# Router logits from four column tiles of TensorE, with the router's weights stationary and one turn of the result

## The reference, cut to what matters

```python
h = _layernorm(x) * (1 + ca) + sa
x = x + ga * mamba(h)                      # a scan over 2048 steps for 512 x 16 states
h = _layernorm(x) * (1 + cb) + sb
s_raw_MN = h @ Wg_DN                       # router logits, 8 a token: what the change touches
routed = softmax(s_raw_MN[:, :7]); shared = softmax(s_raw_MN[:, 7:])
mask = one_hot(top_k(routed, 1)); sel = routed * mask
gates = concatenate([sel / sum(sel), shared / sum(shared)])
y = sum over n of gates[:, n] * ((silu(h @ W1_n[:, H:]) * (h @ W1_n[:, :H])) @ W2_n)
x = x + gb * y
```

## Time and profile before

| what | value |
|---|---|
| time, median of 3 | 2514.27 us |
| the profiled execution's own time | 2508.63 us |
| its span, first to last instruction | 2506.6 us |
| mean granted TensorE clock | 0.904 |
| VectorE busy | 1929.8 us (77%) |
| GpSimd busy | 1955.7 us (78%) |
| TensorE busy | 2176.9 us (87%) |
| ScalarE busy | 1360.7 us (54%) |
| one chunk, mean of 14 | 117.0 us |

### The profile page before, as it was taken

The page is one execution under the profiler, slowest core; times in us unless marked ns, Lnnn a source line. Parts: engine busy times, 40 slices in busy tenths (PEclk is TensorE's granted clock), DMA queues, the critical chain, the costliest instruction groups (busy, mean ns, idle before and its releaser), DMA issues. The chain is left out here.

```text
span 2506.6 us, 31126 instructions
## 1 busy us (share of the span) xinstructions
PE 2176.9 (87%) x7664; PEld 1058.5 (42%) x7665; DVE 1929.8 (77%) x2060; ACT 1360.7 (54%) x2440; POOL 1955.7 (78%) x840
## 2 busy tenths in 40 slices
PE   8769898988989898999898898989857649999997
PEld 3214343443434343434343443434323335566654
DVE  2799999999999999989999999999897162222222
ACT  3666666667575766666666667576644232222221
POOL 1999889898989898988989898989897014555553
PEclk9868989898989898988989898989878869999999
DMA  5443242424232333424242424232321062222221
GB/s 154 135 110 94 76 103 67 101 68 113 81 92 74 96 82 87 116 79 105 68 103 69 101 68 111 81 94 77 89 68 42 24 208 76 85 84 83 87 85 45
DMA packets 149401, 224.39 MB, mean 90 GB/s; under 512 B 48227, under 2 KB 85617, under 8 KB 145138
## 3 DMA queue, kind: packets, MB, share of 16 engines
q1 hardware_dynamic: 135858, 182.44, 28.0%
q0 software_dynamic: 13376, 40.12, 5.2%
HBM read 99.48 MB, written 31.47 MB: 52 GB/s over the span
## 5 line engine op out<-in xcount | busy, mean ns | idle before, releaser
L1023 POOL TENSOR_TENSOR hs<-hs,c_rep 128x2048 f32<-128x2048 f32 x256 | 1154.5, 4528 | 37.3 <-ACT state L767 37.2
L863 DVE TENSOR_TENSOR_SCAN hs<-dA,state,hs 128x512 f32<-128x512 f32 x768 | 931.1, 1264 | 21.0 <-ACT dA L747 16.7
L747 ACT ACTIVATE dA<-d_rep,a 128x512 f32<-128x512 f32 x1024 | 690.0, 686 | 427.7 <-DVE hs L863 423.2
L1016 POOL TENSOR_TENSOR hs<-u_rep,b_rep 128x2048 f32<-128x2048 f32 x96 | 435.5, 4536 | 88.9 <-PE bank L517 88.9
L850 DVE TENSOR_TENSOR hs<-u_ps,b_rep 128x2048 f32<-128x2048 f32 x160 | 360.9, 2272 | 8.0 <-issue 4.8
L488 PE MATMUL bank<-n,w1s 128*128 128x512 f32 x512 | 268.4, 661 | 68.0 <-DVE delta L831 39.2
L863 DVE TENSOR_TENSOR_SCAN hs<-dA,hs 128x512 f32<-128x512 f32 x256 | 294.0, 1202 | 19.7 <-ACT dA L747 18.6
L517 PE MATMUL bank<-hs,spread 128*32 128x512 f32 x2048 | 280.3, 696 | 32.1 <-POOL hs L1023 28.0
L1408 DVE TENSOR_TENSOR hid<-z,sg 128x512 f32<-128x512 f32 x70 | 48.4, 692 | 298.1 <-ACT sg L1386 298.1
L1326 PE MATMUL z<-w1r,hT 128*128 x560 | 260.5, 608 | 3.4 <-issue 2.4
L446 PE MATMUL bank<-xin,w_in 128*128 128x512 f32 x512 | 245.1, 619 | 9.2 <-ACT xin L600 9.2
(11 more groups left out here) (173 smaller groups left out, 2531.9 us busy)
## 6 DMA issues: line engine op xcount, KB each, us to landing
d_rep<-delta SPq DMA_DIRECT2D x1024, 64.0 KB, 2.0
u_rep<-us SPq DMA_DIRECT2D x384, 64.0 KB, 2.0
b_rep<-bc_rows SPq DMA_DIRECT2D x64, 256.0 KB, 4.7
c_rep<-bc_rows SPq DMA_DIRECT2D x64, 256.0 KB, 7.8
xres<-in_x SPq DMA_DIRECT2D x16, 512.0 KB, 3.6
token_rows<-xpad SPq DMA_DIRECT2D x32, 256.0 KB, 2.3
token_rows<-xres SPq DMA_DIRECT2D x16, 512.0 KB, 3.0
xin<-in_x SPq DMA_DIRECT2D x15, 512.0 KB, 9.5
```

The costliest lines, as they stand in the source:

```text
L747: nc.scalar.activation(dA[:, u % ABANK, :], d_rep[:, q, :], ACT.Exp, scale=t["a"][:, u:u + 1]).then_inc(da_ready, 1)
L863: nc.vector.tensor_tensor_scan(hs[:, s % RING, g, :], dA[:, u % ABANK, :], hs[:, s % RING, g, :], state[:, u:u + 1] if m else 0.0, ALU.mul ...
L1016: nc.gpsimd.tensor_tensor(hs[:, s % RING], u_rep[:, i % UBUF, :].unsqueeze(1).to_broadcast([P, NG, T]), b_rep[:, par, :].rearrange("p (g t ...
L1023: nc.gpsimd.tensor_tensor(hs[:, s % RING, :, :], hs[:, s % RING, :, :], c_rep[:, par, :].rearrange("p (g t) -> p g t", g=NG), ALU.mult).th ...
```

## The change

- `GL` now holds the router's 8 columns stationary and lets 128 tokens of `h2T` move. Tile tt of the tokens goes to column tile tt of the array (32 columns, of which 8 are used), and its logits come out on partitions 32 tt to 32 tt + 7, one partition for each expert, one column for each token. It is 8 matmuls as before, ordered with the feature halves outside. The bank's other partitions hold what was in them.
- ScalarE copies all 128 partitions x 128 columns of this to `lgT`, the first 128 columns of `hid`'s part 1.
- `GT` is a new TensorE group: one transpose of `lgT` gives tokens on partitions. It stands between `B` 0 and `B` 1 in the plan.
- ScalarE copies from it the 4 x 8 columns of `lg`, at `evict[10][3]` ahead of `B` 1, where `logits_kept` is signalled now; the copy at the old place, `evict[10][0]`, signals `lgT_ready`.
- `GT` reads through ScalarE, so the list of such groups has 29 members, and every one after `GT` gets the other of the two banks.

```diff
+        lgT = hid[:, 1, 0:P]
+        lgT_made, lgT_ready = sem("lgT_made"), sem("lgT_ready")
         plan:
-            9: [(('GL', 0), -1), (('RB', 1), -1), (('SUM', 1), 0), (('B', 0), -1), (('B', 1), -1), (('B', 2), -1), (('DB', 0), 1), (('B', 3), -1), (('DT', 2), 1)],
+            9: [(('GL', 0), -1), (('RB', 1), -1), (('SUM', 1), 0), (('B', 0), -1), (('GT', 0), -1), (('B', 1), -1), (('B', 2), -1), (('DB', 0), 1), (('B', 3), -1), (('DT', 2), 1)],
         evict:
-            10: [[(('GL', 0), -1), (('L0', 0), 1), (('RB', 1), -1)], [], [(('B', 0), -1)], [(('B', 1), -1)]],
+            10: [[(('GL', 0), -1), (('L0', 0), 1), (('RB', 1), -1)], [], [(('B', 0), -1)], [(('GT', 0), -1), (('B', 1), -1)]],
-        ACT_READS = ("T", "XS", "CV", "RS", "XP", "DT", "T2", "RB", "GL", "B")
+        ACT_READS = ("T", "XS", "CV", "RS", "XP", "DT", "T2", "RB", "GL", "GT", "B")
         made: "GL": logits_made -> "GL": lgT_made, "GT": logits_made
         kept: "GL": logits_kept -> "GL": lgT_ready, "GT": logits_kept
         TensorE:
                 elif kind == "GL":
                     pe.wait_ge(h2T_ready, KD * f + KD)
-                    for tt in range(TT):
-                        for k in range(KD):
-                            last = nc.tensor.matmul(ps_[:, tt * NEXP:(tt + 1) * NEXP], h2T[:, k, tt * P:(tt + 1) * P], t["wg"][:, k, :],
-                                                    start=(k == 0), stop=(k == KD - 1))
+                    for k in range(KD):
+                        for tt in range(TT):
+                            last = nc.tensor.matmul(ps_[DS * tt:DS * tt + NEXP, 0:P], t["wg"][:, k, :], h2T[:, k, tt * P:(tt + 1) * P],
+                                                    start=(k == 0), stop=(k == KD - 1), skip_group_check=True, tile_position=(0, DS * tt))
+                elif kind == "GT":
+                    pe.wait_ge(lgT_ready, f + 1)
+                    last = nc.tensor.transpose(ps_[:, 0:P], lgT, t["ident"][:])
         ScalarE:
                 elif kind == "GL":
+                    nc.scalar.activation(lgT, ps_[:, 0:P], ACT.Copy).then_inc(lgT_ready, 1)
+                elif kind == "GT":
                     if not (known(f) and f == 0):
                         act.wait_ge(logits_stored, 16 * f)
-                    nc.scalar.activation(lg[:], ps_[:, 0:TT * NEXP].rearrange("p (t e) -> p t e", t=TT), ACT.Copy).then_inc(logits_kept, 1)
+                    nc.scalar.activation(lg[:], ps_[:, 0:P].rearrange("p (t e) -> p t e", t=TT)[:, :, 0:NEXP], ACT.Copy).then_inc(logits_kept, 1)
```

More of the change, by code:

```diff
@@ L206, in fused_program @@
                  ("DT", 0), ("DT", 1), ("DB", 0), ("DT", 2), ("DT", 3), ("DB", 1), ("RS", 0), ("DB", 2), ("RS", 1), ("DB", 3), ("RS", 2), ("RS", 3)]
-        ACT_READS = ("T", "XS", "CV", "RS", "XP", "DT", "T2", "RB", "GL", "B")
+        ACT_READS = ("T", "XS", "CV", "RS", "XP", "DT", "T2", "RB", "GL", "GT", "B")
         made = {"T": turned, "XS": xs_made, "RS": res_made, "CV": conv_made, "XP": xdbl_made, "DT": dt_made, "DB": db_made, "SUM": y_ready, "OP": out_made,
-                "T2": turned2, "RB": back_made, "GL": logits_made, "B": b_made, "A": a_made, "Y": out2_made}
+                "T2": turned2, "RB": back_made, "GL": lgT_made, "GT": logits_made, "B": b_made, "A": a_made, "Y": out2_made}
         kept = {"T": hT_ready, "XS": xs_ready, "RS": res_pre, "CV": us_pre, "XP": xdbl_ready, "DT": exp_ready, "DB": delta_ready, "SUM": yg_ready, "OP": x1_ready,
-                "T2": h2T_ready, "RB": back_kept, "GL": logits_kept, "B": b_kept, "A": hid_ready, "Y": acc_ready}
+                "T2": h2T_ready, "RB": back_kept, "GL": lgT_ready, "GT": logits_kept, "B": b_kept, "A": hid_ready, "Y": acc_ready}
         many = {"T": KD, "XS": KI, "RS": KI, "CV": KI, "XP": 1, "DT": KI, "DB": KI, "SUM": KI, "OP": 2,
-                "T2": KD, "RB": 2, "GL": 1, "B": KI, "A": KI, "Y": 2}
+                "T2": KD, "RB": 2, "GL": 1, "GT": 1, "B": KI, "A": KI, "Y": 2}
         FRONT = ("T", "XS", "CV", "RS", "XP", "DT", "DB")
```

## The result

The changed kernel takes 2485.89 us, the median of 4 runs (2482.32 to 2486.2), beside 2514.02 us for the kernel before on the same chip. The ratio is 0.9882 with a 95% interval of 0.9865 to 0.9899: 28 us faster. The prediction said 14 us faster, 2500 us; the time lies just inside its range of 2483 to 2517 us, but the gain is twice the one forecast. The profiled execution took 2482.32 us (span 2480.3), 26.3 us under that of before.

What follows compares the result with a forecast made beforehand. VectorE paces the kernel, its idle time set by TensorE's line to `SUM` 1. 1.7 us gained less 0.85 lost over 15 chunks (12.8 us), plus 1.2 us at the end, gives 14 us: 2500 us, range 2483 to 2517.

Steps and rivals of the forecast that it cites:

- `SUM` 1's end sets VectorE, GpSimd and ScalarE off: In every chunk three engines wait behind TensorE's line up to `SUM` 1, so TensorE's time there is the chunk's time.
- The logits' 1.04 us: Router logits group on TensorE: forecast to take 1.1 us from first start to last end, instead of 3.58 us.
- The bank as the change's own cost: Behind `SUM` 1, `B` 1 waits for `B` 0's copy; its own copy comes 0.95 us late, VectorE loses 0.85 us a chunk.
- `GT` and both copies hidden: `GT`'s turn and ScalarE's two copies fall into waits around `B` 0 and `B` 1; 0.2 us if the second's cover went.
- The rival of the tiles one by one: Logits group: column tiles don't run together, 2532 us; chance 0.13, shared with a second late copy a chunk.
- the clock takes it back: Shorter chunks put the clock's rise later within `SUM` 1, costing another 0.8 us a chunk: 2509 to 2514 us; chance 0.24.
- I take 1.7 us: Gain a chunk assumed to reach `SUM` 1's end, out of a 2.1 us earlier start.
- a switch of tile layout: Ahead of `RB` 1, TensorE changes from column tiles to the whole array: 0.29 us a switch.
- the rise follows: Clock's rise keeps its distance from `SUM` 1's start, so all 2.1 us arrive at its end.
- the rise stays: Clock's rise stays at its moment in time during `SUM` 1, so only 1.05 us arrive.
- more arrives: Clock rises sooner around `SUM` 1 and VectorE uses all its 3.1 us a chunk: 35 us, 2479 us; chance 0.13.
- paced by the same delayed scans: Readers of `B` 2, `DB` 0, `B` 3 and the next u fan-out, each 0.95 us later, were given no extra cost.

Runs made afterwards that it cites:

- the half and the quarter of the old form: Kernel before, old logits group cut to 4 matmuls (half) or 2 matmuls (quarter), the rest left out: 2486.53 us and 2471.46 us.
- the third bank: Changed kernel with `GT` in the bank of `SUM`, `DB`, `A`, `Y`, so `B` 1 to `B` 3 keep their old banks: 2466.12 us, ratio 0.9814.
- the banks alone: Kernel before, old logits, no `GT`, only the banks of `B` 1 and all groups behind it exchanged: 2529.82 us, ratio 1.0067.
- the eleven traces above: Six traces with the new logits form, five with the old, whole or cut: `SUM` 1 lasts 4.86 to 5.11 and 5.19 to 5.47 us.
- the changed kernel's second trace: Changed kernel run again as it is, for a side-by-side comparison on one chip: 2484.89 us, ratio 0.9884.
- the doubled group: Changed kernel with the new logits group made twice: 2486.27 us, ratio 0.9899.
- `DT` 0 twice: Changed kernel with `GT` in the bank of `SUM`, `DB`, `A`, `Y`, and `DT` 0 made twice in its bank: 2467.78 us, ratio 0.9819.

## Why the prediction was off by half

Right: that `SUM` 1's end sets VectorE, GpSimd and ScalarE off, and that time won there is time won for the chunk (shown by the half and the quarter of the old form: one for one in VectorE's idle time up to there, 1.36 of 1.73 and 2.30 of 2.47 us in the chunk's length). The logits' 1.04 us (forecast 1.1). The bank as the change's own cost, with its place and mechanism (the third bank, and the banks alone): `B` 1's copy 0.95 us late, as worked out, and VectorE's wait 0.76 us for 0.85. `GT` and both copies hidden; the gate step 3.5 us behind the logits (3.4 forecast), the store covered. The rival of the tiles one by one is out: they do run together, 16 loads in 0.55 us and 16 matmuls in 1.04 us. So is the rival that the clock takes it back: the rise came no later after `SUM` 1's start, but sooner.

The Trainium skill, TensorE: Matmul & The Clock Gate, section Part 3: Packing small matmuls — row/col tiling, has loads overlap with matmuls in flight only in other row groups. By the traces that doesn't hold for these column tiles, which share all rows.

Wrong was one term of the sum: "I take 1.7 us". It measured 2.73 us of VectorE's idle time, and `SUM` 1 ended 2.85 us sooner (+9.84 to +6.99). Two things were undersized in it. The start came 2.44 us sooner, not 2.1: I counted `RB` 1's first load as exposed before its matmul, but both are recorded from 1168.11 on, 0.98 us behind the logits' start, where I had 1.25 for the matmul. The 0.29 us that I gave a switch of tile layout came of comparing a load's start without a switch with a matmul's behind one. Matmul with matmul, the next group starts 0.14 us before the last one's end without a switch (1185.00 to 1184.86) and 0.06 us with one (1168.17 to 1168.11): 0.08 us.

The larger one is the clock. I took a value near the middle of "the rise follows" (2.1) and "the rise stays" (1.05), and had read only two of the 15 chunks for it, which are the two extremes: the rise came 2.98 and 4.80 us after `SUM` 1's start there, 3.56 on the mean. The rise did follow, and a little more: on the mean it comes 2.74 us after `SUM` 1's start, and `SUM` 1 lasts 4.97 instead of 5.38 us. So the 1.15 us between 1.7 and 2.85 are 0.34 for the start, 0.40 for what I had taken off for the clock, and 0.41 for the shorter `SUM` 1, which goes with the new form's moving columns (the eleven traces above). 15 x (2.73 - 1.7) = 15 us, against the 14 us between forecast and result. The rival "more arrives" was the nearer one: the rise came sooner, and 2.73 of VectorE's 3.41 us of idle time up to there were used, where the rival had 3.1 (the two waits that it names, 0.60 and 2.61, add up to 3.2). I gave it 0.13. The range held the result only because it had been stretched towards that rival.

Too small was also the bank's price, in the other direction: 0.85 us a chunk, 13 us, where the comparisons give 18 to 20. The 0.8 us at the place foreseen were right, the 0.4 us elsewhere weren't in my sum. The 0.44 us in the table's third row are something else. They are a wait of up to 0.99 us for u's fan-out. In nine of the 14 chunks this fan-out runs at the low clock and takes 2.07 us. In the other five it runs at full clock, takes 1.12 us, and nobody waits; the last two rows are from one of these.

```profile
1193.50 2.07 PE L512 MATMUL u_ps<-us,spread 32*128 32x512 f32 x2
...
1195.61 2.29 DVE L857 TENSOR_TENSOR hs<-u_ps,b_rep 128x2048 f32<-128x2048 f32 x1 [0.99 <-PE u_ps L512]
...
848.11 1.12 PE L512 MATMUL u_ps<-us,spread 32*128 32x512 f32 x2
...
849.35 2.26 DVE L857 TENSOR_TENSOR hs<-u_ps,b_rep 128x2048 f32<-128x2048 f32 x1
```

I had called this reader "paced by the same delayed scans". That held for the nearest fan-out (for set 12), not for this one, the next (GpSimd makes the input of set 13 itself). The bank makes it start 0.9 us later behind `SUM` 1, but whether VectorE waits 0.8 to 1.0 us for it or not at all goes by the clock. With the banks alone it does so in two of 14 chunks, in the changed kernel's second trace in six, with the doubled group in 13. It is there with the old banks too, once in the third bank's trace and three times in that of the quarter on the kernel before. So this row is where the clock's low stretch falls, and no price of the bank by itself.

Over the whole kernel, by the profiled executions: the 14 chunks gave 20.9 us where the forecast has 14 x 0.85 = 11.9, the stretch between the last two groups 3.0 instead of 0.85, and the two ends 2.4 instead of 1.2: 26.3 instead of 14 us.

Why the rise follows `SUM` 1 so closely is open. That it moves with the chunk's length is seen (the banks alone: 2.0 to 5.1 us), as is that a doubled group pulls it by 0.4 us; neither was taken apart further.

## What to carry to other kernels

Read a disputed clock in all the repetitions of a stage, not in two, before halving a gain for it; here the gain of an earlier start arrived one for one at the stage's end. Where buffers go by position modulo a small number, a small new member between two large ones puts these on the same buffer: give it a buffer of its own, which here was worth 19 us on top of the change's 28. And where one operand has few columns (here the router's 8), hold it stationary on column tiles if the turn of the result can be hidden: 3.58 us became 1.04, and the turn cost nothing that could be measured.

## What the runs showed of the hardware

Loads of weights into one column tile overlap with matmuls of the others over the same rows: the changed kernel's 16 loads lie within 0.55 us, with the first matmuls in flight from the same moment on (1167.13). Between column tiles and the whole array TensorE lost little: the next group's first matmul begins 0.06 us before the last one's modelled end (1168.17 to 1168.11), as at the other switches, and 0.14 us before it without a switch. Extra work of 0.9 us in a gap of 2.8 us, ending 8.8 us ahead of `SUM` 1, did nothing for the clock there (`DT` 0 twice), while 0.85 us more of moving columns on all four column tiles right ahead of it brought the rise 0.4 us sooner.
